# Spreading the sixteen row maxima of an attention step over twelve slots in place of eleven

## The chip, the core and the metric

The kernel runs on one core of a Trainium2 chip. The metric is the device time of one execution in microseconds, lower is better. A core has a matrix engine (TensorE, in the profile PE, its weight loads PEld), a vector engine (VectorE, DVE), an engine for activations (ScalarE, ACT), a general one (GpSimd, POOL) and one that mostly issues DMAs (SyncE, SP). Each has an in-order queue, and they meet through semaphores.

## What is computed

Two attention blocks, one after the other, over x of 16 batches x 512 positions x 512 features, both with float32 inputs. The change lies in the first one, with 16 heads of 32 features:

```python
xn = layer_norm(x, norm_w, norm_b)
q = (xn @ q_w + q_b).reshape(Bx, Tx, H, -1)
k = (xn @ k_w + k_b).reshape(Bx, Tx, H, -1)
att = jnp.einsum('bnhl,bmhl->bnmh', q, k)
att = att + (1.0 - mask) * -1000000.0        # mask over n, the query position
att = jax.nn.softmax(att, axis=2)
v = ((xn @ v_w + v_b) * src_mask[:, :, None]).reshape(Bx, Tx, H, -1)
y = jnp.einsum('bnmh,bmhl->bnhl', att, v).reshape(Bx, Tx, Dx)
```

Behind it come a layer norm of y with a scale and a shift from a condition vector, a silu, an output projection and the residual; the second block is a linear attention.

## The kernel before

Two phases run one behind the other. The first, attention_phase, computes q, k, v, the softmax and its product with v for all 16 batches and writes y to DRAM; the second, projection_phase, does the rest and is not touched.

In the first phase a batch b has four steps g = 0 to 3, each for a group of four heads (HG=4), and a step has 16 slots (SLOTS). The loops over steps are the same on every engine; each engine's queue walks through the same slots and does its own part. A step has these strands:

- **Exponents** (exp_scores, L537): one matmul of 512 columns in a slot, transposed scores, less the row maxima that ride along as two extra rows (the shift rows) of the stacked operand q_stack. ACT exponentiates the bank (L769) into probs. The step's own exponents begin in slot 3 (LAG); slots 0 to 2 finish those of the step before. There are two exp_banks: a matmul waits until ACT has read the one before the last.
- **Maxima for the next step** (max_scores, L522): 16 matmuls, four heads by four tiles of positions. DVE reduces each bank to one column of negmax (maximum, L905). There are two max_banks: matmul m waits for the reduce of m-2. How many fall in which slot is said by maxima(k), the subject of the change: the first of a slot is issued after the exponent matmul, the second after all other work of the slot.
- **The turning of the maxima** (transpose_max, L528): in slot MAX_TURN, after the exponent matmul, PE turns negmax (128x16) into a work bank. It waits for all 16 reduces. DVE splits it in two parts (split_shift, L916 and L918) and SP writes them as the shift rows of the next step (L345), which that step's first exponent waits for in its slot 3.
- **Projections** (project_quarter, L505): q and k for the step after next, a quarter (three matmuls of 512 columns) in each of slots 0 to 3 and 4 to 7. ACT writes the high part of each (L743) and issues two DMAs into the stacks (L750), DVE writes the low part (L891). In the steps g=3 and g=0 two tiles of v as well, one in slots 8, 9, 10 and 10, one (called v') in slots 13, 14, 15 and 15. DVE adds the bias of the first in slot 11, behind the slot's maxima, and of the second at the end of the step (add_value_bias, L900); ACT then multiplies by the mask (L755, the first in slot 12).
- **x of the next batch**, in g=1: DVE normalises it in slots 5 to 8 (L880), PE turns its four tiles in slots 8 to 11 (transpose_x, L512), ACT copies the high part (L737) and DVE takes the low part a slot later (L886).
- **Weighted values** (weigh_values, L548) and **sums** (L560): 16 and 4 short matmuls behind the exponent of slot 9 (two tiles of the step before, and its sums), 16 more behind that of slot 11. The sums use an addition that GpSimd makes (L293).

Projections, turned x and turned maxima take the two work banks in turn, in the order of uses_of. Each use, before its first matmul, waits in take_bank until the use before the last has been read:

```python
if static >= 2:
    pe.wait_ge(work_read, number - 1)
```

In g=0 the order is q, k, v2, m, v3, in g=3 q, k, v0, m, v1, in g=1 q, k, x0 to x3, m, and in g=2 q, k, m (m is the turned maxima). So v3 waits until v2's bias add has read its bank, and in g=1 m waits for the low part of x2.

Of the kernel before, what the change touches and what calls it, by code (L numbers as in the profile page):

```python
# [35 lines left out]
SLOTS = TT * HG  # L36
# [68 lines left out]
def attention_phase(nc, shared, x, mask, mask1, norm_w, norm_b, q_w, q_b, k_w, k_b, v_w, v_b, cond, films, b_vectors,  # L105
# [4 lines left out]
    with ExitStack() as ctx:  # L110
# [126 lines left out]

        QUARTERS = {"q": (0, 1, 2, 3), "k": (4, 5, 6, 7), "v": (8, 9, 10, 10), "v'": (13, 14, 15, 15)}
        X_TURNS = (8, 9, 10, 11)
        MAX_TURN = 12  # L240

        FILM_TURNS = ((4, 6, 8), (6, 8, 12))
        FIRST_V_BIAS = {1: 0, 3: 1, 5: 2, 7: 3}
# [1 line left out]

        def maxima(k):

            return range(min(k * 3 // 2, SLOTS), min((k + 1) * 3 // 2, SLOTS))

        def exp_of(b, g, k):  # L250

# [5 lines left out]
        def use(b, g, what, last=False):  # L257

            n = len(FIRST_USES) + sum(len(uses_of(h, last)) for h in range(g)) + uses_of(g, last).index(what)
            return n, b * USES + n  # L260
# [218 lines left out]
        def _(pe):  # L479
# [35 lines left out]
            def max_scores(b, g, m, first=False):  # L515

                j, nt = m // TT, m % TT
                if m == 0:
                    pe.wait_ge(stack_in[g], DMA * STACK_DMAS * (b + 1))
                if not (first and m < 2):  # L520
                    pe.wait_ge(max_done, SLOTS * step_of(b, g) + m - 1)
                pe.matmul(max_bank[m % 2][:, :], q_stack[0:ROWS_MAX, g, j, nt * P:(nt + 1) * P],  # L522
                          k_stack[0:ROWS_MAX, g, j, :], start=True, stop=True).then_inc(max_full, 1)

            def transpose_max(b, g, number):
                out = take_bank(number)
                pe.wait_ge(max_done, SLOTS * (step_of(b, g) + 1))
                pe.transpose(out[0:SLOTS, 0:P], negmax[:, :], ident[:, :]).then_inc(work_full, 1)  # L528
# [142 lines left out]
            def step(b, g, last=False, first=False):  # L671
# [3 lines left out]
                for k in range(SLOTS):  # L675
# [3 lines left out]
                    if has_next:  # L679
                        for m in maxima(k)[:1]:  # L680
                            max_scores(n_b, n_g, m)
                        if k == MAX_TURN:
                            transpose_max(n_b, n_g, use(b, g, "m", last))
# [31 lines left out]
                    if has_next:  # L715
                        for m in maxima(k)[1:]:
                            max_scores(n_b, n_g, m)
# [145 lines left out]
        def _(dve):  # L863
# [31 lines left out]
            def add_value_bias(b, mt, static, number):  # L895
                dve.wait_ge(work_full, number + 1)
                if not (type(b) is int and b == 0):

                    dve.wait_ge(pv_done, TT * (step_of(b, 0) - 1) + mt + 1)
                dve.tensor_tensor(v_sb[:, mt, :], work_bank[static % 2][:, :], v_bias[:, :], ALU.add  # L900
                                  ).then_inc(work_read, 1)
# [6 lines left out]
            def split_shift(b, g, static, number):  # L908

                s = step_of(b, g)  # L910
                dve.wait_ge(work_full, number + 1)
                if not (type(s) is int and s == 0):

                    p_b, p_g = (b, g - 1) if g else (b - 1, NG - 1)
                    dve.wait_ge(shift_in[p_g], 2 * DMA * (p_b + 1))
                dve.tensor_copy(shift[:, 0, :], work_bank[static % 2][0:SLOTS, 0:P]).then_inc(shift_hi, 1)  # L916
                dve.wait_ge(shift_hi, s + 1)
                dve.tensor_tensor(shift[:, 1, :], work_bank[static % 2][0:SLOTS, 0:P],  # L918
                                  shift[:, 0, :].bitcast(F32), ALU.subtract).then_inc(work_read, 1)
# [105 lines left out]
            def step(b, g, last=False):  # L1025
                has_next = not last or g < NG - 1
                n_b, n_g = (b, g + 1) if g + 1 < NG else (b + 1, 0)
                for k in range(SLOTS):
                    if has_next:
                        for m in maxima(k):  # L1030
                            maximum(n_b, n_g, m)
                    for i, what in enumerate("qk"):
                        if k == QUARTERS[what][-1] + 1 and (not last or g < NG - 2):
                            low_of(what, (g + 2) % NG, use(b, g, what, last)[0], high_count(b, g, i))
                    if g == 1 and not last and 5 <= k < 5 + TT:
                        normalise_x(b + 1, [k - 5])
                    if g == 1 and not last and k - 1 in X_TURNS:
                        tt = X_TURNS.index(k - 1)
                        low_of_x(tt, use(b, 1, f"x{tt}")[0], high_count(b, 1, 2 + tt))
                    if k == 11 and (g == 0 or (g == NG - 1 and not last)):  # L1040
                        mt = 2 if g == 0 else 0
                        add_value_bias(b if g == 0 else b + 1, mt, *use(b, g, f"v{mt}", last))
                    if has_next and k == MAX_TURN:
                        split_shift(n_b, n_g, *use(b, g, "m", last))
                    if g == 0 and not last and k == 13:
                        statistics_of_x(b + 1)
                    if last and g == NG - 2 and k == FILM_TURNS[0][2] + 1:
                        add_film_bias(0, use(b, g, "film0c", last))
                    if last and g == NG - 1:
                        for half in range(2):  # L1050
                            if k == FILM_TURNS[1][half] + 1:
                                copy_film_half(1, half, use(b, g, "film1" + "ab"[half], last))
                        if k == FILM_TURNS[1][2] + 1:
                            add_probs(dve, step_of(b, g), 1)
                            add_film_bias(1, use(b, g, "film1c", last))
                            finish_film()
# [736 lines left out]
def build(nc, i, out):  # L1793

    B = i["x"].shape[0]
    yT_dram = nc.dram_tensor("yT_scratch", (B, D, T), F32, kind="Internal").ap()
    sums_dram = nc.dram_tensor("sums_scratch", (B, NG * HG, T), F32, kind="Internal").ap()
    mb0_dram = nc.dram_tensor("mask_bias0_scratch", (B, 2, T), F32, kind="Internal").ap()
    mb1_dram = nc.dram_tensor("mask_bias1_scratch", (B, T), F32, kind="Internal").ap()
    mask1 = i["mask_BxSx1_fk1"].rearrange("b t o -> b (t o)")  # L1800
    films = [tuple(i[layer + n] for n in names) for layer, names in
             (("L0_cond_", ("emb_w", "emb_b", "sb_norm_w", "sb_norm_b")), ("L1_cond_", ("W_emb", "b_emb", "ln2_w", "ln2_b")))]
    b_vectors = films[0][1:] + films[1][1:] + (i["L1_cond_ln_w"], i["L1_cond_ln_b"], i["L1_cond_bk"])
    with ExitStack() as ctx:
        shared = Shared(nc, ctx, B)
        attention_phase(nc, shared, i["x"], i["mask_BxS_ff1"], mask1, i["L0_cond_norm_w"], i["L0_cond_norm_b"],
                        i["L0_cond_q_w"], i["L0_cond_q_b"], i["L0_cond_k_w"], i["L0_cond_k_b"], i["L0_cond_v_w"],
                        i["L0_cond_v_b"], i["cond_2048"], [film[0] for film in films], b_vectors,
                        yT_dram, sums_dram, mb0_dram, mb1_dram)
        projection_phase(nc, shared, i["x"], i["L0_cond_out_w"], i["L0_cond_out_b"], i["L1_cond_Wq"], i["L1_cond_bq"],  # L1810
                         i["L1_cond_Wk"], i["L1_cond_Wv"], i["L1_cond_bv"], i["L1_cond_W_out"], i["L1_cond_b_out"],
                         yT_dram, sums_dram, mb1_dram, out)
# [17 lines left out]
```

## Time and profile before

| what | value |
|---|---|
| time, median of 3 runs | 2792.67 us (2791.71 to 2795.97) |
| profiled execution, its own time | 2797.07 us |
| its span | 2795.2 us |
| PE busy | 2672.4 us, 96% |
| DVE busy | 1827.3 us, 65% |
| POOL busy | 1352.2 us, 48% |
| ACT busy | 1223.7 us, 44% |
| mean granted clock of PE | 0.982 |

The profile is of one execution. Busy time counts overlapping stretches of an engine once; matmuls are pipelined, so the start times of two neighbours say more of their cost than their durations (0.40 us each where they start 0.23 us apart). The first phase ends at about 1541 us of the span.

### The profile page before, as it was taken

What the parts mean: (1) busy time and instruction counts of PE and PEld (TensorE: products, weight loads), DVE (VectorE), ACT (ScalarE), POOL (GpSimd) and SP (SyncE); (2) the same over time, 40 slices, a digit from 0 to 9 for tenths busy, and PEclk for the clock granted to TensorE, in tenths of its full rate; (3) what the DMA queues carried; (4) which work ended last, traced back from release to release, by engine and by line L of the source; (5) the groups of instructions that cost most, each with busy time, mean ns of one, the idle gap of its engine ahead of it and who ended that gap; (6) DMA issues with size and microseconds to landing.
All of it is one profiled execution on the core that took longest, in us unless ns stands there. A gap on an engine that the chain in (4) does not pass through costs nothing. (4 is left out here: it accounts for less than half of the span.)

```text
span 2795.2 us, 43889 instructions
## 1 busy us (share of the span) xinstructions
PE 2672.4 (96%) x13890; PEld 1947.1 (70%) x13890; DVE 1827.3 (65%) x3272; ACT 1223.7 (44%) x2039; POOL 1352.2 (48%) x604
## 2 busy tenths in 40 slices
PE   7999999999999999999998699999999999999997
PEld 4666556665666666666663488888888888888886
DVE  6766666666665666666653666666677776776674
ACT  3555555555555555555554323333333333333332
POOL 1656566656666665666564234433333333343432
PEclk9999999999999999999998699999999999999998
DMA  6656665666566656666564411111111111111100
GB/s 138 100 79 99 99 99 78 99 99 99 78 98 98 97 80 96 96 95 95 81 99 137 145 35 50 49 49 49 49 49 47 48 45 37 43 45 49 34 30 31
DMA packets 114915, 211.44 MB, mean 76 GB/s; under 512 B 12408, under 2 KB 14508, under 8 KB 114876
## 3 DMA queue, kind: packets, MB, share of 16 engines
q1 hardware_dynamic: 78012, 143.81, 22.3%
q10 hardware_dynamic: 36864, 67.13, 18.2%
q8 instruction: 22, 0.36, 0.1%
q14 instruction: 17, 0.14, 0.0%
HBM read 74.87 MB, written 34.18 MB: 39 GB/s over the span
## 5 line engine op out<-in xcount | busy, mean ns | idle before, releaser
L905 DVE TENSOR_REDUCE negmax<-max_bank 128x1 f32<-128x512 f32 x1024 | 682.1, 687 | 330.2 <-PE max_bank L522 328.7
L769 ACT ACTIVATE probs<-exp_bank 128x512 f32<-128x512 f32 x1024 | 586.8, 596 | 538.0 <-PE exp_bank L537 484.6
L293 POOL TENSOR_TENSOR probs_sum<-probs_sum,probs 128x2048 f32<-128x2048 f32 x126 | 581.0, 4611 | 73.6 <-ACT probs L769 69.5
L293 POOL TENSOR_TENSOR probs_sum<-probs 128x2048 f32<-128x2048 f32 x63 | 288.4, 4577 | 541.1 <-ACT probs L769 541.1
L537 PE MATMUL exp_bank<-q_stack,k_stack 100*128 100x512 f32 x1024 | 432.5, 432 | 24.5 <-ACT probs L769 21.8
L522 PE MATMUL max_bank<-k_stack,q_stack 98*128 98x512 f32 x1024 | 421.4, 416 | 21.6 <-DVE negmax L905 12.6
L537 PEld LDWEIGHTS exp_bank<-q_stack,k_stack 100*128 100x128 f32 x1024 | 193.5, 189 | 171.2 <-ACT probs L769 85.3
L522 PEld LDWEIGHTS max_bank<-k_stack,q_stack 98*128 98x128 f32 x1024 | 192.7, 190 | 139.2 <-issue 59.3
L1528 POOL TENSOR_TENSOR sT_lo<-silu,sT_hi 128x512 fp32r<-128x512 f32 x128 | 173.0, 1372 | 175.2 <-DVE sT_hi L1643 175.2
L548 PE MATMUL y_bank<-probs,v_sb 128*32 128x512 f32 x2048 | 248.0, 602 | 0.0
L1309 PE MATMUL b_work<-ident,area 128*128 128x128 f32 x1536 | 193.0, 281 | 25.1 <-DMA b_sums<-sums_scratch 13.3
L1283 PE MATMUL b_work<-b_wout_hi,sT_hi 128*128 128x512 f32 x512 | 201.8, 394 | 9.5 <-issue 5.0
L1309 PEld LDWEIGHTS b_work<-ident,area 128*128 128x128 f32 x1536 | 176.1, 145 | 39.4 <-DMA b_sums<-sums_scratch 14.3
L1283 PE MATMUL b_work<-b_wout_lo,sT_hi 128*128 128x512 f32 x512 | 201.1, 393 | 0.0
L1283 PE MATMUL b_work<-b_wout_hi,sT_lo 128*128 128x512 f32 x512 | 201.1, 393 | 0.0
L1523 POOL TENSOR_TENSOR rstd_y<-var_eps_y,b_minus_half 128x4 f32<-128x4 f32 x32 | 32.8, 1024 | 334.1 <-DVE var_eps_y L1607 334.1
L1643 DVE CAST sT_hi<-silu 128x512 fp32r<-128x512 f32 x128 | 102.1, 818 | 104.0 <-ACT silu L1468 104.0
L1507 ACT ACTIVATE area<-area 128x512 f32<-128x512 f32 x64 | 40.4, 632 | 274.6 <-POOL area L1573 274.6
L1468 ACT ACTIVATE silu<-b_work,film_b,film_a 128x512 f32<-128x512 f32 x128 | 93.2, 777 | 128.7 <-PE b_work L1309 101.2
L1543 POOL TENSOR_TENSOR result<-area,row_out 128x512 f32<-128x512 f32 x64 | 82.8, 1304 | 125.9 <-DMA out_x<-result 125.9
L548 PEld LDWEIGHTS y_bank<-probs,v_sb 128*32 128x32 f32 x2048 | 53.6, 109 | 120.0 <-issue 112.7
L1494 ACT ACTIVATE area<-area,kmax 128x512 f32<-128x512 f32 x64 | 46.0, 720 | 196.8 <-DVE kmax L1669 196.6
(194 smaller groups left out, 5290.1 us busy)
## 6 DMA issues: line engine op xcount, KB each, us to landing
q_stack<-q_stage ACTq DMA_DIRECT2D x128, 256.0 KB
k_stack<-k_stage ACTq DMA_DIRECT2D x128, 256.0 KB
x_sb<-in_x SPq DMA_DIRECT2D x16, 1024.0 KB, 5.6
q_stack<-q_stage SPq DMA_DIRECT2D x64, 256.0 KB
k_stack<-k_stage SPq DMA_DIRECT2D x64, 256.0 KB
yT_scratch<-y_stage SPq DMA_DIRECT2D x64, 256.0 KB
area<-yT_scratch SPq DMA_DIRECT2D x16, 1024.0 KB, 5.2
area<-in_x SPq DMA_DIRECT2D x64, 256.0 KB, 2.8
```

The lines of the kernel that those rows point to most:

```text
L293: eng.tensor_tensor(probs_sum[:, :, :], so_far, probs[:, mt, :, :], ALU.add).then_inc(probs_added, 1)
L522: pe.matmul(max_bank[m % 2][:, :], q_stack[0:ROWS_MAX, g, j, nt * P:(nt + 1) * P], k_stack[0:ROWS_MAX, g, j, :], start=True, stop=True).th ...
L537: pe.matmul(exp_bank[k % 2][:, :], k_stack[0:ROWS_EXP, g, j, mt * P:(mt + 1) * P], q_stack[0:ROWS_EXP, g, j, :], start=True, stop=True).th ...
L548: last = pe.matmul(y_bank[DH0 * j:DH0 * (j + 1), :], v_sb[:, mt, P * j + DH0 * g:P * j + DH0 * (g + 1)], probs[:, mt, j, :], start=(mt == ...
L769: act.activation(probs[:, mt, j, :], exp_bank[k % 2][:, :], ACT.Exp).then_inc(exp_done, 1)
L905: dve.tensor_reduce(negmax[:, m:m + 1], max_bank[m % 2][:, :], AXX, ALU.max, negate=True).then_inc(max_done, 1)
L1283: last = pe.matmul(out, lhs(a, kt), rhs(c, kt), start=(kt == 0 and a + c == 0), stop=(kt == KT - 1 and a == 1))
L1309: last = pe.transpose(out[:, i * P:(i + 1) * P], src(i), ident[:, :])
L1468: act.activation(silu[:, kt % SILUS, :], bank(u), ACT.Silu, scale=film_columns(film_a[film], kt, row), bias=film_columns(film_b[film], kt, ...
L1528: pool.tensor_tensor(sT_lo[:, kt, :], silu[:, kt % SILUS, :], sT_hi[:, kt, :].bitcast(F32), ALU.subtract).then_inc(sT_lo_done, 1)
L1543: pool.tensor_tensor(result[:, tt, :], x_sb[:, tt, :], rows["out1"][:, :], ALU.add).then_inc(result_biased, 1)
L1643: dve.tensor_copy(sT_hi[:, kt, :], silu[:, kt % SILUS, :]).then_inc(sT_hi_done, 1)
```

## The change

Two lines of attention_phase. maxima(k) gave slots 0 to 10 the counts 1,2,1,2,1,2,1,2,1,2,1; it gives slots 0 to 11 the counts 1,1,2,1,1,2,1,1,2,1,1,2. The maxima are turned in slot 13 in place of 12. Both PE and DVE take their order from these lines.

```diff
-        MAX_TURN = 12
+        MAX_TURN = 13
...
         def maxima(k):
 
-            return range(min(k * 3 // 2, SLOTS), min((k + 1) * 3 // 2, SLOTS))
+            return range(min(k * 4 // 3, SLOTS), min((k + 1) * 4 // 3, SLOTS))
```

## Rows read from the trace of the kernel before

**Rows 1.** The page: PE's busy time, and the granted clock by slice.

```profile
PE 2672.4 (96%) x13890; PEld 1947.1 (70%) x13890; DVE 1827.3 (65%) x3272; ACT 1223.7 (44%) x2039; POOL 1352.2 (48%) x604
...
PEclk9999999999999999999998699999999999999998
```

**Rows 2.** Windows of steps g=0 to 3: busy us of each engine, clock, DMA share.

```profile
520.36:544.33 23.97, 23.97 (x123) 15.96 (x122) 16.36 (x31) 12.71 (x22) 13.84 (x4) 1.00 0.56 79
544.33:567.79 23.46, 21.57 (x115) 12.97 (x113) 17.80 (x31) 13.09 (x24) 13.81 (x5) 1.00 0.56 79
567.79:588.05 20.26, 19.43 (x97) 11.42 (x97) 12.44 (x20) 11.05 (x19) 13.70 (x3) 1.00 0.64 85
588.05:612.02 23.97, 23.96 (x121) 16.04 (x122) 13.15 (x21) 12.27 (x21) 14.88 (x5) 1.00 0.69 129
```

**Rows 3.** Timeline of PE in step g=0: start us, us, engine, line, operation.

```profile
520.36 0.40 PE L537 MATMUL exp_bank<-q_stack,k_stack 100*128 100x512 f32 x1
...
525.03 0.39 PE L505 MATMUL work_bank<-xT_hi,wq_lo 128*128 128x512 f32 x1
...
528.15 0.49 PE L537 MATMUL exp_bank<-q_stack,k_stack 100*128 100x512 f32 x1
...
540.31 0.50 PE L537 MATMUL exp_bank<-q_stack,k_stack 100*128 100x512 f32 x1
540.65 0.27 PE L528 MATMUL work_bank<-ident,negmax 128*16 128x128 f32 x1
...
540.99 0.40 PE L505 MATMUL work_bank<-wv_hi,xT_hi 128*128 128x512 f32 x1
...
544.33 0.40 PE L537 MATMUL exp_bank<-q_stack,k_stack 100*128 100x512 f32 x1
```

**Rows 4.** Timeline of DVE in the same step: last reduces, bias add.

```profile
536.50 1.29 DVE L905 TENSOR_REDUCE negmax<-max_bank 128x1 f32<-128x512 f32 x2 [0.24 <-PE max_bank L522]
538.45 0.69 DVE L900 TENSOR_TENSOR v_sb<-work_bank,v_bias 128x512 f32<-128x512 f32 x1 [0.67 <-PE work_bank L505]
```

**Rows 5.** Timeline of ACT in the same step, slots 4 to 6.

```profile
527.50 1.78 ACT L769 ACTIVATE probs<-exp_bank 128x512 f32<-128x512 f32 x3 [1.35 <-PE exp_bank L537]
```

**Rows 6.** Timeline of PE in steps g=1 and g=2.

```profile
555.71 0.50 PE L522 MATMUL max_bank<-k_stack,q_stack 98*128 98x512 f32 x1 [0.31 <-DVE negmax L905]
...
559.53 0.50 PE L522 MATMUL max_bank<-k_stack,q_stack 98*128 98x512 f32 x1
...
562.09 0.66 PE L512 MATMUL work_bank<-ident,x_sb 128*128 128x128 f32 x4 [0.78 <-DVE xT_lo L886]
...
564.76 0.66 PE L512 MATMUL work_bank<-ident,x_sb 128*128 128x128 f32 x4
...
567.79 0.50 PE L537 MATMUL exp_bank<-q_stack,k_stack 100*128 100x512 f32 x1 [0.20 <-ACT probs L769]
...
581.87 0.74 PE L522 MATMUL max_bank<-k_stack,q_stack 98*128 98x512 f32 x2
...
583.15 0.50 PE L522 MATMUL max_bank<-k_stack,q_stack 98*128 98x512 f32 x1 [0.31 <-DVE negmax L905]
...
585.68 0.50 PE L537 MATMUL exp_bank<-q_stack,k_stack 100*128 100x512 f32 x1
...
588.05 0.50 PE L537 MATMUL exp_bank<-q_stack,k_stack 100*128 100x512 f32 x1 [0.19 <-ACT probs L769]
```

**Rows 7.** Timeline of DVE in steps g=1 and g=2.

```profile
561.35 0.68 DVE L886 TENSOR_TENSOR xT_lo<-work_bank,xT_hi 128x512 fp32r<-128x512 f32 x1
...
582.41 1.98 DVE L905 TENSOR_REDUCE negmax<-max_bank 128x1 f32<-128x512 f32 x3 [1.91 <-PE max_bank L522]
```

**Rows 8.** The shift rows' DMAs (L345), all 128: issue to landing.

```profile
DMA to landing us min/median/max: 1.8/1.9/9.1
```

**Rows 9.** Windows over one PV product each, at the two granted clocks.

```profile
1537.00:1540.40 3.40, 3.40 (x17) 0.74 (x20) 2.47 (x2) 0.73 (x2) 0.00 (x0) 0.50 0.00 0
538.40:540.30 1.90, 1.90 (x17) 0.42 (x16) 0.69 (x1) 1.08 (x2) 1.90 (x1) 1.00 0.49 79
```

## Prediction

> **What bounds the kernel now.** I read the page's busy shares first, then its 40 slices. TensorE (PE) is busy for 96% of the span and holds nine tenths or more in nearly every slice at the full granted clock [rows 1]. So a microsecond counts only if it adds work to PE's queue or holds that queue up. The windows of the four group steps of one middle batch come next [rows 2]: 23.97 us (g=0), 23.46 (g=1), 20.26 (g=2) and 23.97 (g=3), with PE busy all through the first and the last, and idle 1.89 and 0.83 us in the others. The two long steps carry the V tiles (I call them V steps), g=1 the turning of x, g=2 neither. The change touches these steps alone, some 62 of them. The second phase, after about 1550 us, is untouched.
>
> Then the order of time on PE within a V step [rows 3]. Streaming matmuls start 0.2335 us apart: 20 of them lie between 520.36 and 525.03. I call this a unit. Slots 12 to 15 run from 540.31 to 544.33: the exponent matmul of slot 12 is at 540.31, the turning of the maxima at +0.34 with no idle time shown before it, the first V' matmul at +0.68, and the next step's first matmul at +4.02. The turning waits for nothing because its last maximum was computed in slot 10, and slot 11's PV product (16 short matmuls, from 538.4 to 540.3 in the second of [rows 9]) gave VectorE (DVE) 1.9 us to reduce it. DVE had finished its reduces by 537.79 and the V bias add by 539.14 [rows 4], before the turning.
>
> **What the change does to the order.** Before, slots 0 to 10 compute 1,2,1,2,1,2,1,2,1,2,1 maxima. After, slots 0 to 11 compute 1,1,2,1,1,2,1,1,2,1,1,2. Nothing is added or removed: 16 max matmuls, 16 reduces, one turning, the split and two shift rows remain. What moves: slots 0 to 7 hold 10 maxima in place of 12; slots 8 to 10 hold four both times; slot 11 now holds maxima 14 and 15, and they are issued behind its PV product. Slot 12 has a single exponent matmul, and the turning stands behind slot 13's. The cover of the PV product is gone. On DVE, whose queue is in order, the reduces of 14 and 15 now stand ahead of slot 11's V bias add (V steps) and of the low part of x2 (g=1).
>
> **The tail of a V step.** Let P be the time at which PE is through slot 11's PV product, 540.31 in rows 3. Max 14 starts at P and max 15 a wait-free 0.33 later. The same pair behind a long product is seen in g=2 (x2 in one row): first matmul at 581.87 [rows 6], first reduce at 582.41 [rows 7], 0.54 later. Two back-to-back reduces take 1.29 [rows 4], so the second ends at P+1.83. A waiting PE goes on 0.06 after DVE ends: the low part ends at 562.03 [rows 7] and the matmul behind it starts at 562.09 [rows 6]. The turning therefore starts at P+1.89, not P+0.34. PE has only the two max and two exponent matmuls to do before (to about P+1.1).
>
> Worse stands behind it. V' goes into the work bank that the earlier V tile used, which is free only when the bias add has read it. That add now starts one pitch after the second reduce. Of two reduces in 1.29 with 0.69 each the second starts 0.60 after the first, so the add starts at P+0.54+1.20 = P+1.74 and takes 0.69 (the add in rows 4): it ends at P+2.43, and V' starts at P+2.49. From V' to the next step PE took 544.33-540.99 = 3.34 [rows 3]. The next step starts at P+5.83 where it was P+4.02: **+1.81**, the two moved matmuls (0.47 of work) included. ScalarE (ACT) has the mask multiply of slot 12 behind the same add, to about P+3.2, then exponent 13 to P+3.7. PE wants that bank in slot 15, at P+4.15, so this second wait stays covered.
>
> **What slots 0 to 7 give back.** Two matmuls fewer are 0.47. But PE's exponent of slot 6 already waits for ACT: the last q matmul is at 525.03, the q high part and its DMA issues hold ACT, slot 4's exponential starts at 527.50 [rows 5] and ends near 528.09, and PE goes on at 528.15 [rows 3], 3.12 us after 525.03 where 13 units are 3.04. One of the two maxima leaves exactly that stretch: 12 units are 2.80 and the exponent still can't start before 3.12. It only makes the wait longer. The other leaves slots 6 and 7, where nothing waits. So 0.24 comes back. **V step: 1.81-0.24 = +1.57.** The 16 steps g=0 and 15 of g=3 have V: 31 x 1.57 = **+48.7 us**.
>
> **g=2.** Slots 0 to 7: -0.24. Slot 8 gets a second max, +0.23. Behind the sums PE did max 13, max 14, exponent 10, max 15 and exponent 11 in slots 9 and 10. Max 15 came at 583.15 [rows 6], behind a wait for the reduce of max 13. Now these are max 12, exponent 10, max 13 and exponent 11, with no pair and no wait: 0.33 and two units, 0.80 from the first to exponent 11. Before it was 583.15+0.34-581.87 = 1.62. That is -0.82. P itself is thus earlier by 0.83. In the tail the turning starts at P+1.89 again and slot 14's exponent behind it at P+1.93. Its ACT pass starts 0.54 later, takes 0.60, and the next step's first exponent, which wants the same bank, starts at P+3.1; before, 588.05-585.68 = 2.37. That is +0.73. **-0.10 each, 15 times: -1.5 us**.
>
> **g=1.** Slots 0 to 7: -0.24, and some 0.16 less of short waits for DVE. Slot 8 loses a wait for DVE of 0.31 (555.71 [rows 6], some 0.37 with what a stop costs beside it) and gains one matmul behind a turning (0.30). Behind the sums (Q = 559.53) the turning of x2 waited for DVE until Q+2.56, because reduces 13 and 14 stood ahead of x0's low part. Now one reduce does: it ends at Q+1.2, the low part at Q+1.83, x2 starts at Q+1.89: -0.67. In the tail the turning needs the bank that x2's low part frees, now behind both reduces. With x3 between them, max 15 is at P+0.73, its reduce ends at P+1.89, the low part at P+2.5, the turning starts at P+2.56, and the next step at P+3.8 by the same chain as in g=2; before, 567.79-564.76 = 3.03. That is +0.77. **-0.37 each, 15 times: -5.6 us**. The last batch's g=1 and g=2 I take as zero.
>
> **Where the shift rows go.** Their two DMAs follow the split on SP's queue, with nothing between, and land in 1.9 us [rows 8]. They are wanted in slot 3. In g=2 I estimate the turning at P+1.89, the split and the two issues 1.8 us more, the landing near P+5.6; slot 3's exponent comes 16 units after the step's first, at P+6.8. In the V steps it comes at P+9.6, with over 3 us to spare. So they cost nothing. GpSimd (POOL) adds the exponentials somewhat later, but PE wants these sums only behind slot 9 of the next step.
>
> **Sum.** 48.7-1.5-5.6 = +41.6 us. The profiled execution took 2797.07 us (span 2795.2), 4.4 above the median of 2792.67; from it 2838.7, and from the median **2834.3 us**, 1.5% slower. About 0.2% is what a measurement can tell here.
>
> **Bounds.** A V step: +1.2 if slots 0 to 7 give back the full 0.47 and slot 15's small wait goes too; +1.9 if nothing comes back. g=1: -0.8 to 0. g=2: -0.4 to +0.3. Low: 31x1.2-15x1.2 = +19; high: 31x1.9+15x0.3 = +63.
>
> **Rivals.** (a) *The late reduce is covered and the smoother order wins.* If the turning and V' found DVE ready, the tails would cost only the moved matmuls (0.47 each), and per batch the rest gives 0.24+0.24+1.24+0.83 = 2.55 against 4x0.47 = 1.88: -0.67, times 15.5 is -10 us, 2782. It decides if DVE's second reduce and the add end before about P+1.1. Rows 6 and 7 speak against it: 0.54 and 1.29 can't fit. 4%. (b) *The V bank is not what V' waits for*, and the turning alone costs: V' then comes 0.34 behind it, at P+2.23, the V step is +1.31, and the sum 31x1.31-7 = +34, 2826. It decides if the bias add is through by P+2.2. In rows 4 add and reduces are far apart, so no row shows their pitch; 12%. *An exact cancel* has half of (a)'s gap closed, 3%. (c) *The shift rows come late* in g=1 and g=2, where cover is 0.9 to 1.2 us. Landing took up to 9.1 us at worst [rows 8]. One us over the cover in both is 30 us more, 2864. The rows' DMAs meet little traffic at the step's end, hence 4%. (d) *The clock falls.* At the lower granted level 17 matmuls of PV take 3.40 us, at full 1.90 [rows 9]. If the 14 matmuls behind the wait ran so in each V step: 31x3.3 = 102 us more, 2937. Against it: g=1 idles 1.89 us at 1.00 [rows 2], and the longest new gap is about 1. 2%. The Trainium skill's page "TensorE: Matmul & The Clock Gate", section "HAM oscillation — how this bites in real kernels", warns that waits between bursts of matmuls can throttle the clock again and again; the trace of this stage doesn't show that, and the sum above leaves it out. The forecast has 75%.
>
> **Range.** 2814 to 2852 leaves out (a), the cancel, (c) and (d), and holds (b). Faster 0.04, same 0.03, slower 0.93.
>
> **What would show it.** Windows of the four steps near 25.5, 23.1, 20.2 and 25.5 us. L528 no longer free of idle time but released by the DVE reduce L905 (g=0,2,3) or the low part L886 (g=1); V' matmuls (L505) released by DVE L900; the DVE wait at max 15 and most of the x2 wait gone; the exponent of slot 6 waiting some 0.3 us for ACT; the split L916 some 1.5 us or more after exponent 13. It would be wrong if V steps stay under 24.5, or if PE waits for the shift DMA in every batch.

## The result

The changed kernel takes 2852.97 us (median of 4 runs, 2850.51 to 2855.16) against 2792.19 us for the kernel before: ratio 1.0215, 95% interval 1.0197 to 1.0232, 60.8 us slower. I had forecast 2834.3 us with a range up to 2852.0. The direction was right, the size 18.7 us short, and the time lies just outside the range. Each time here and below is the median of a kernel's undisturbed runs; two of the twelve of experiment 9, at 3785 and 5289 us, are left out.

### The profile page after: what moved, and what is told of

It is laid out like the page before. It is cut to its first block and busy times, and to the rows that moved or that the text cites. A ratio compares the mean times of both kernels' runs of the same rounds, so it can differ in the third digit from the quotient of the medians.

```text
span 2852.8 us, 43889 instructions
## 1 busy us (share of the span) xinstructions
PE 2684.6 (94%) x13890; PEld 1953.7 (68%) x13890; DVE 1824.6 (64%) x3272; ACT 1225.1 (43%) x2039; POOL 1351.4 (47%) x604
## 5 line engine op out<-in xcount | busy, mean ns | idle before, releaser
L905 DVE TENSOR_REDUCE negmax<-max_bank 128x1 f32<-128x512 f32 x1024 | 690.3, 688 | 524.1 <-PE max_bank L522 523.4
L537 PE MATMUL exp_bank<-q_stack,k_stack 100*128 100x512 f32 x1024 | 413.9, 420 | 28.6 <-ACT probs L769 25.5
L1309 PEld LDWEIGHTS b_work<-ident,area 128*128 128x128 f32 x1536 | 176.1, 145 | 39.2 <-DMA b_sums<-sums_scratch 14.3
```

The source lines that it names most:

```text
L537: pe.matmul(exp_bank[k % 2][:, :], k_stack[0:ROWS_EXP, g, j, mt * P:(mt + 1) * P], q_stack[0:ROWS_EXP, g, j, :], start=True, stop=True).th ...
L905: dve.tensor_reduce(negmax[:, m:m + 1], max_bank[m % 2][:, :], AXX, ALU.max, negate=True).then_inc(max_done, 1)
L1309: last = pe.transpose(out[:, i * P:(i + 1) * P], src(i), ident[:, :])
```

## The profile after

The page's busy shares and slices, as in [rows 1]:

```profile
PE 2684.6 (94%) x13890; PEld 1953.7 (68%) x13890; DVE 1824.6 (64%) x3272; ACT 1225.1 (43%) x2039; POOL 1351.4 (47%) x604
...
PEclk9999999999999999999999699999999999999998
```

The work is the same to the instruction, the span 57.6 us longer (2852.8), so the difference is waiting or clock. The slices of the clock look as before; at 70 us each they hide what follows. Windows of the steps g=0 to g=3 of one batch, with a second g=2 at the end (span us, then busy us of each engine with counts, granted clock, DMA share, GB/s), as in [rows 2]:

```profile
538.82:564.52 25.70, 24.55 (x122) 15.91 (x121) 16.50 (x31) 12.87 (x22) 13.79 (x4) 1.00 0.52 74
564.52:587.44 22.92, 20.84 (x114) 12.74 (x113) 17.47 (x29) 13.02 (x24) 13.58 (x5) 1.00 0.58 80
587.44:609.12 21.68, 20.41 (x97) 12.51 (x97) 12.47 (x20) 10.99 (x20) 13.75 (x3) 0.92 0.60 79
609.12:634.90 25.78, 24.61 (x122) 16.14 (x123) 13.16 (x21) 12.34 (x21) 15.18 (x4) 1.00 0.67 120
...
492.79:513.00 20.21, 18.93 (x97) 11.38 (x97) 12.46 (x20) 11.01 (x20) 13.77 (x3) 1.00 0.64 84
```

The two V steps are 1.7 to 1.8 us longer than in [rows 2], g=1 is 0.5 us shorter, an undisturbed g=2 nearly as long as before (20.21 against 20.26 us). But one g=2 took 21.68 us, at a mean granted clock of 0.92. That wasn't in my sum.

The tail of a V step on PE (start us, us, engine, line), to hold against [rows 3]:

```profile
556.83 1.92 PE L548 MATMUL y_bank<-probs,v_sb 128*32 128x512 f32 x16
558.68 0.73 PE L522 MATMUL max_bank<-k_stack,q_stack 98*128 98x512 f32 x2
559.26 0.63 PE L537 MATMUL exp_bank<-q_stack,k_stack 100*128 100x512 f32 x2
560.57 0.28 PE L528 MATMUL work_bank<-ident,negmax 128*16 128x128 f32 x1 [0.68 <-DVE negmax L905]
561.16 0.50 PE L505 MATMUL work_bank<-wv_hi,xT_hi 128*128 128x512 f32 x1 [0.32 <-DVE v_sb L900]
...
564.52 0.40 PE L537 MATMUL exp_bank<-q_stack,k_stack 100*128 100x512 f32 x1
```

and on DVE in the same stretch, to hold against [rows 4]:

```profile
559.22 1.29 DVE L905 TENSOR_REDUCE negmax<-max_bank 128x1 f32<-128x512 f32 x2 [3.21 <-PE max_bank L522]
560.43 0.68 DVE L900 TENSOR_TENSOR v_sb<-work_bank,v_bias 128x512 f32<-128x512 f32 x1
```

P is 558.68. The first reduce starts at P+0.54, the turning at P+1.89, V' at P+2.48, the next step at P+5.84. The forecast had 0.54, 1.89, 2.49 and 5.83. The two brackets are the two stops of the forecast. DVE, which had been done before P, now has three operations in a row there, and PE waits for the second and the third.

Where the forecast was off in a V step lies ahead of P. The exponents of slots 2 and 6 on PE, to hold against [rows 3]:

```profile
540.92 0.40 PE L505 MATMUL work_bank<-xT_hi,wq_lo 128*128 128x512 f32 x1
541.20 0.50 PE L537 MATMUL exp_bank<-q_stack,k_stack 100*128 100x512 f32 x1
541.53 0.39 PE L522 MATMUL max_bank<-k_stack,q_stack 98*128 98x512 f32 x1
...
543.63 0.39 PE L505 MATMUL work_bank<-xT_hi,wq_lo 128*128 128x512 f32 x1
...
546.20 0.39 PE L522 MATMUL max_bank<-k_stack,q_stack 98*128 98x512 f32 x1
546.74 0.50 PE L537 MATMUL exp_bank<-q_stack,k_stack 100*128 100x512 f32 x1 [0.16 <-ACT probs L769]
```

and on ACT:

```profile
544.77 1.21 ACTq L750 DMA_DIRECT2D q_stack<-q_stage  x2
546.09 1.79 ACT L769 ACTIVATE probs<-exp_bank 128x512 f32<-128x512 f32 x3 [1.35 <-PE exp_bank L537]
```

The maximum and the exponent of slot 6 start 0.54 us apart where streaming takes 0.23: PE waits for the exponential that stands behind the two DMA issues. From the step's first matmul to P it was 540.31-520.36 = 19.95 before [rows 3] and is 558.68-538.82 = 19.86: the two missing maxima give back 0.09, not 0.24. Slot 6 isn't the reason: its exponent starts 3.11 us behind the last q matmul (546.74-543.63), where the forecast had 3.12. The missing 0.15 lies in slot 2. Its exponent starts 0.28 behind the matmul ahead of it, and the next one 0.33 behind it, where streaming takes 0.23 each. In the kernel before one maximum more stood ahead of it, and it streamed:

```profile
522.93 0.40 PE L537 MATMUL exp_bank<-q_stack,k_stack 100*128 100x512 f32 x1
523.17 0.39 PE L522 MATMUL max_bank<-k_stack,q_stack 98*128 98x512 f32 x1
```

The stop in g=1, and what came behind it:

```profile
583.62 0.50 PE L522 MATMUL max_bank<-k_stack,q_stack 98*128 98x512 f32 x1
583.95 0.60 PE L512 MATMUL work_bank<-ident,x_sb 128*128 128x128 f32 x4
584.31 0.48 PE L522 MATMUL max_bank<-k_stack,q_stack 98*128 98x512 f32 x1
584.63 0.63 PE L537 MATMUL exp_bank<-q_stack,k_stack 100*128 100x512 f32 x2
586.25 0.27 PE L528 MATMUL work_bank<-ident,negmax 128*16 128x128 f32 x1 [0.99 <-DVE xT_lo L886]
586.28 0.71 PE L537 MATMUL exp_bank<-q_stack,k_stack 100*128 100x512 f32 x2
587.44 0.50 PE L537 MATMUL exp_bank<-q_stack,k_stack 100*128 100x512 f32 x1 [0.45 <-ACT probs L769]
...
588.84 0.63 PE L505 MATMUL work_bank<-xT_hi,wq_lo 128*128 128x512 f32 x1
589.26 0.63 PE L537 MATMUL exp_bank<-q_stack,k_stack 100*128 100x512 f32 x1
...
591.39 0.42 PE L537 MATMUL exp_bank<-q_stack,k_stack 100*128 100x512 f32 x1
```

P is 583.62 here. The turning starts at P+2.63 (forecast 2.56), the next step at P+3.82 (3.8). From about 588.0 the matmuls start 0.42 to 0.43 us apart until 591.39. A window over that stretch:

```profile
588.00:591.40 3.40, 3.40 (x10) 2.62 (x9) 1.39 (x2) 1.17 (x2) 3.40 (x1) 0.51 0.04 10
```

The granted clock is at its lower level, 1.2 GHz. PE had stopped twice just before, for 0.99 and 0.45 us. In the stretch from 100 us to 1480 us the changed kernel shows ten such falls of 3.4 us, the kernel before none. (In the last batch, which has less work, both kernels show one of 10.2 us. In the kernel before it begins at 1486.2 us, behind a wait of 2.86 us for a stack.) Seven of the ten lie behind the tail of g=1, three behind that of g=2, none behind a V step, and a step that has one is 1.5 us longer (g=2 21.71 against 20.18). The tail of a g=2 has two stops as well, the first of them shorter:

```profile
607.92 0.28 PE L528 MATMUL work_bank<-ident,negmax 128*16 128x128 f32 x1 [0.67 <-DVE negmax L905]
...
609.12 0.50 PE L537 MATMUL exp_bank<-q_stack,k_stack 100*128 100x512 f32 x1 [0.43 <-ACT probs L769]
```

The count is of the one execution that was profiled. The mean granted clock of the changed kernel's four runs is 0.977 to 0.979, that of experiment 7, which has no such fall, 0.983 to 0.985. From this I estimate some 8 to 12 falls in each run.

The balance, from the lengths of all steps in the trace (here and in the experiments from the first maximum of a step to that of the next, which differs from the windows by up to 0.1 us): V steps 31 x 1.71 = 53.0; g=1 15 x -0.52 = -7.8; g=2 15 x -0.09 = -1.4; ten falls x 1.5 = 15.0. That is 58.8 of a difference of 57.6 us; the small rest is at the start and end of the phase.

## The experiments

The theory: a V step pays for the last two reduces and the bias add once PV no longer covers them, and the stops of g=1 and g=2 let the clock fall. The rivals: the turning's place costs by itself; the spread costs by itself; the falls have another reason.

**1. The turning in slot 13 alone**, on the kernel before.

```diff
-        MAX_TURN = 12
+        MAX_TURN = 13
```

> Kernel before, with the turning moved to slot 13 alone; the maxima stay in eleven slots. Theory (the order of the last two maxima and the PV product is what costs): reduce 15 is through long before slot 13, so no wait, V steps stay at 23.97 us, the time at 2792 us within 5, and the granted clock does not fall in the middle of the first phase. Rival (a turning one slot later costs by itself, through the bank or the shift rows): 10 us or more slower.

Measured: 2793.59 us, ratio 1.0001 (0.9990 to 1.0011). V steps 23.97 and 23.99 us, no fall of the clock between 100 and 1480 us. The second line of the change costs nothing.

**2. The spread alone**, the turning left in slot 12.

```diff
         def maxima(k):
-            return range(min(k * 3 // 2, SLOTS), min((k + 1) * 3 // 2, SLOTS))
+            return range(min(k * 4 // 3, SLOTS), min((k + 1) * 4 // 3, SLOTS))
```

> The new spread with the turning left in slot 12. Theory: the turning waits until the same moment (1.9 us behind the PV product) but exponent 13 now stands behind it; V steps stay at 25.7 us (V' waits for its bank anyway), g=1 and g=2 are 0.6 us longer each, some 18 us over the changed kernel, 2871 us, and the granted clock falls at least as often. Rival (the wait is the turning's place, not the maxima's): faster than the changed kernel.

Measured: 2853.37 us, ratio 1.0213 (1.0196 to 1.0231), as slow as the whole change. The steps are as expected, V steps 25.6 to 25.7, g=1 23.55 and g=2 20.7, which is 0.5 us more each. But the clock fell twice, not ten times, which gives back nearly all of that; here the expectation missed. So the slot of the turning decides nothing about the V steps: both stops come from where the last two maxima stand. And a longer stop doesn't bring more falls: the turning of g=1 waits 1.22 us here, that of g=2 0.91, and the stop behind each is 0.45 and 0.46 as before.

**3. PV behind slot 11's maxima.** The new spread and slot 13 stay; PE issues the product last in its slot.

```diff
@@ exp_slot
-                if e == 8:
-                    weigh_values(b, g, 0)
-                    weigh_values(b, g, 1)
@@ step, behind the second maximum of the slot
+                    if k == LAG + 8:
+                        weigh_values(b, g, 0)
+                        weigh_values(b, g, 1)
```

> The new spread and slot 13, but on PE slot 11's PV product is issued behind that slot's maxima instead of ahead of them. Theory: the product covers the reduces of 14 and 15 again, no wait before the turning or V', V steps 23.9 us, g=1 23.1, g=2 20.5 (max 15 now waits for reduce 13), no fall of the clock in the phase: 2787 us. Rival (the spread itself costs, whatever stands behind it): near the changed kernel, 2840 or more.

Measured: 2802.05 us, ratio 1.0032 (1.0021 to 1.0042). 51 of the 61 us are gone with one moved product. The turning waits no more, and the clock doesn't fall before the last batch. The line of the turning:

```profile
L528 PE MATMUL work_bank<-ident,negmax x64: 269/273/273, 63.8 to 1517.7; 128*16 128x128 f32 x64
its engine sat idle before it (us, times) until:
  issue: 0.6, 1
  DVE negmax L905: 0.2, 1
```

In the changed kernel the same row says 99.7 us of idle time in 105 intervals (weight load and matmul counted apart) until DVE's reduces and 16.1 until the low part. Still it is 8 us slower than the kernel before, measured beside it (2793.94), and 15 us slower than I expected. The V steps are 24.42 and 24.26 us, not 23.9; g=1 is 22.99 and g=2 20.65 us. A part of that is my slip: I counted what slots 0 to 7 give back and not the 0.47 us that the same two matmuls take in slot 11. The window of one:

```profile
522.58:547.00 24.42, 24.26 (x123) 15.84 (x122) 16.26 (x28) 12.70 (x22) 13.82 (x4) 1.00 0.55 78
```

Slots 0 to 7 take 10.40 us with 42 matmuls here (522.58 to 532.98) and took 10.46 with 44 before. The smoother order gives almost nothing back in a V step even where its tail is covered. So rival (a) doesn't come true here; experiment 8 shows what it takes.

**4. The bias add ahead of the reduces** on DVE in slot 11; all else as changed.

```diff
                 for k in range(SLOTS):
+                    if k == 11 and (g == 0 or (g == NG - 1 and not last)):
+                        mt = 2 if g == 0 else 0
+                        add_value_bias(b if g == 0 else b + 1, mt, *use(b, g, f"v{mt}", last))
                     if has_next:
                         for m in maxima(k):
                             maximum(n_b, n_g, m)
...
-                    if k == 11 and (g == 0 or (g == NG - 1 and not last)):
-                        mt = 2 if g == 0 else 0
-                        add_value_bias(b if g == 0 else b + 1, mt, *use(b, g, f"v{mt}", last))
```

> The changed kernel with DVE's slot 11 bias add ahead of the slot's reduces. Theory: V' no longer waits for its bank but follows the turning at P+2.23 in place of P+2.48, V steps 25.45 us, 8 us less in all, 2845 us. If the bank wait were the larger part of a V step's loss: 30 us less.

Measured: 2838.68 us, ratio 1.0162 (1.0145 to 1.0180), 14.3 us less than the changed kernel. V steps are 25.16 to 25.23 us, 0.5 shorter and not 0.25. The falls of the clock are ten, as in the changed kernel. PE in the tail:

```profile
554.12 0.28 PE L528 MATMUL work_bank<-ident,negmax 128*16 128x128 f32 x1 [0.67 <-DVE negmax L905]
554.21 0.49 PE L505 MATMUL work_bank<-wv_hi,xT_hi 128*128 128x512 f32 x1
```

V' starts 0.09 behind the turning, not 0.34. The bank wait is real and its own; I had under-priced it, because the 0.34 from the turning to V' in [rows 3] had an exponent matmul in it as well.

**5. x2's low part ahead of the reduces** on DVE in g=1.

```diff
                 for k in range(SLOTS):
+                    if g == 1 and not last and k == 11:
+                        low_of_x(2, use(b, 1, "x2")[0], high_count(b, 1, 4))
                     if has_next:
                         for m in maxima(k):
                             maximum(n_b, n_g, m)
...
-                    if g == 1 and not last and k - 1 in X_TURNS:
+                    if g == 1 and not last and k - 1 in X_TURNS and k != 11:
```

> The changed kernel with x2's low part ahead of slot 11's reduces on DVE, in g=1. Theory: the turning in g=1 then waits for the reduces alone, P+1.95 in place of P+2.63, and the step is 0.4 us shorter, 6 us in all. If the long stop in g=1 is what lets the clock fall, the ten falls in the middle of the phase go too: 15 us more, 2832 us. Rival (the falls come from the stops as a whole): falls stay near ten, 2847 us.

Measured: 2837.29 us, ratio 1.0164 (1.0146 to 1.0183). g=1 is 22.52 us, 0.5 shorter. The whole is 15.7 us below the changed kernel. Of the falls four are left, all behind g=2 and none behind g=1. So the shorter stop in g=1 ends the falls there, but not those behind g=2: between the theory and the rival. The four runs lie 11 us apart, and the slowest (2845.13 us) has a lower mean clock (0.978) than the profiled one (0.981), so it most likely has more falls.

**6. Unused matmuls in g=1's stop.** They need no bank that is in use and take no wait away.

```diff
+                        if k == MAX_TURN and g == 1 and not last:
+                            pe.wait_ge(max_done, SLOTS * step_of(n_b, n_g) + SLOTS - 1)
+                            for _ in range(4):
+                                pe.matmul(max_bank[0][:, :], q_stack[0:ROWS_MAX, n_g, 0, 0:P],
+                                          k_stack[0:ROWS_MAX, n_g, 0, :], start=True, stop=True)
                         if k == MAX_TURN:
                             transpose_max(n_b, n_g, use(b, g, "m", last))
```

> The changed kernel with four unused matmuls (scores into max bank 0, which the next step overwrites) ahead of the turning in g=1, after the reduce of maximum 14; they fit into the stop and take no wait away. Clock theory: TensorE is busier there, no falls to the lower clock in the middle of the phase, g=1 stays at 23.06 us, 15 us less, 2838 us. Rival (the falls have another reason, or cost nothing): 2853 us or slightly more.

The stop filled, from PE's timeline (the four are L685):

```profile
581.34 0.64 PE L537 MATMUL exp_bank<-q_stack,k_stack 100*128 100x512 f32 x2
581.82 1.09 PE L685 MATMUL max_bank<-k_stack,q_stack 98*128 98x512 f32 x4
582.97 0.27 PE L528 MATMUL work_bank<-ident,negmax 128*16 128x128 f32 x1
```

Measured: 2841.77 us, ratio 1.0167 (1.0151 to 1.0183). The turning is still at P+2.63 and g=1 at 23.05 us. No fall is left behind g=1, but six are there behind g=2, where there had been three. Adding work took 11 us away. The profiled run is the slowest of the four (2844.42 us).

**7. The same in g=1 and g=2** (four and two matmuls):

```diff
-                        if k == MAX_TURN and g == 1 and not last:
+                        if k == MAX_TURN and g in (1, 2) and not last:
...
-                            for _ in range(4):
+                            for _ in range(4 if g == 1 else 2):
```

> The changed kernel with four unused matmuls in the stop before the turning of g=1 and two in that of g=2. With fillers in g=1 alone the falls behind g=1 were gone and six came behind g=2. Clock theory: none is left in the middle of the phase, every step takes its undisturbed length (25.7, 23.05, 20.18, 25.7 us), 2838 us. Rival (the falls only move to another place, the V steps): six or more stay, 2842 us or slower.

Measured: 2838.29 us, ratio 1.0168 (1.0151 to 1.0185). There is no fall between 100 and 1500 us; the steps are 25.7, 23.06, 20.17 and 25.67 us in every batch. With every wait in place the falls alone were worth 2852.97-2838.29 = 14.7 us. What is left is 4 us from my forecast.

**8. ACT's stack DMAs one exponential later**, with PV behind the maxima as in experiment 3.

```diff
                             high_of(what, (g + 2) % NG, number, static)
+                        if k == QUARTERS[what][-1] + 1 and (not last or g < NG - 2):
                             stack_high(what, (g + 2) % NG, high_count(b, g, "qk".index(what)))
```

> The new spread with the PV product behind slot 11's maxima, and in addition ACT issues the two stack DMAs of q and k one exponential later. Theory: in slots 0 to 7 PE waits in slot 6 for the exponential that stands behind ACT's DMA issues, and this wait eats what two fewer maxima give back (slots 0 to 7 took 10.40 us with 42 matmuls, 10.46 with 44). Without it each step is 0.3 us shorter, 19 us in all: 2783 us. Rival (something else holds slots 0 to 7): no change from 2802.

Measured: **2780.60 us, ratio 0.9952 (0.9940 to 0.9964)**, faster than both kernels, and 21.5 us less than experiment 3. V steps 23.93 and 23.85 us, g=1 23.0, g=2 20.2. The exponent of slot 6 had been held by the exponential that stands behind two DMA issues on ACT (1.21 us), and this wait had eaten the gain: slots 0 to 7 of a step g=0 now take 9.95 us, not 10.41. g=1 gains nothing by the move. It was already nearly 0.6 us shorter than in the kernel before in experiment 3, and at 15 steps this is some 8 of the 12 us that the new order is now ahead.

**9. The same on the kernel before.**

> The kernel before with ACT's two stack DMA issues one exponential later. Theory: its wait in slot 6 is only 0.09 us and a dearer start behind it, so 5 us less, 2788 us. Rival (the later stacks are then waited for by the next step): slower.

Measured: 2790.45 us, ratio 0.9993 (0.9984 to 1.0002): no difference that can be measured. Steps are shorter by 0.03 to 0.09 us. The move is worth something only where the spread has made the wait large.

**10. The same on the changed kernel.**

> The changed kernel with ACT's stack DMA issues one exponential later, PV product where the change leaves it. Theory: slots 0 to 7 give back what the two missing maxima are worth, each of the steps is 0.4 us shorter, some 25 us in all, V steps 25.25 us: 2828 us, with the stops of the tail and about as many falls of the clock unchanged. Rival (the gain was special to the kernel without stops in the tail): 2850 us.

Measured: 2851.23 us, ratio 1.0210 (1.0193 to 1.0227), 1.7 us less and not 25. V steps did fall, to 25.26 us, 0.43 x 31 = 13 us. g=1 and g=2 kept their length. Behind g=2 the next step's first maximum now waits for the stack that is loaded later:

```profile
608.38 0.49 PE L522 MATMUL max_bank<-k_stack,q_stack 98*128 98x512 f32 x1 [0.24 <-DMA k_stack<-k_stage]
```

In g=1 slots 0 to 7 do take 0.4 us less, but in slot 8 PE then waits for a reduce: the second maximum starts 0.71 us behind the turning of x ahead of it, where it had been 0.35. And the clock fell in fifteen places, three of them (all behind g=2) for twice as long, where it had been ten. That took back nearly all of what the V steps gave. A gain ahead of a stop can be lost in it.

## Why the prediction was right and wrong

*The tail of a V step* was right to 0.02 us at each of its four points. Its source in the order, the last two maxima behind PV, is shown by experiments 1 to 3. *The split of that loss* between turning and bank was off: the bank add is worth 0.5 us a step (experiment 4), so rival (b)'s price was wrong too, though the sum of both was right.

*"So 0.24 comes back"* failed in size. The wait for ACT in slot 6 came as foreseen (3.11 against 3.12 us), and experiments 3 and 8 show that moving the DMA issues removes it. But in the V step shown 0.09 came back. With one maximum less ahead of it, the exponent of slot 2 in g=0 meets ACT, which is still at the exponentials behind the mask multiply of g=3's second V tile; this costs 0.15 us, which I had not counted. In g=3 the last q matmul comes 0.09 late, nearly all of it in slot 0. At +1.71 against +1.57, 31 steps make 4.3 us.

*g=2* was right (-0.09 against -0.10). *g=1* was -0.52 against -0.37, 2 us in all: slots 0 to 7 gave back 0.29 and not 0.40, but the waits in slot 8 and ahead of x2 shrank by 0.3 more than I had put.

*The shift rows* hid as forecast: two exponents in the whole run waited for them, 2.9 us together (one before, 2.3 us).

*The clock* is the step that failed: the sum had nothing for it. Rival (d) got 2% with the reason "g=1 idles 1.89 us at 1.00 [rows 2], and the longest new gap is about 1". The stop did come out at 0.99 us. The reason was wrong: g=1 idles 2.08 us now (22.92-20.84), hardly more than before. The sum over a step says nothing of it. Before, the x2 stop of 0.78 us [rows 6] stood ahead of a PV product; now the stops stand close together at the end of the step, and the clock falls right behind. That this place makes the difference is my reading; no run tests it by itself. I also looked for the fall in V steps, where V' work follows and it never came. Its real form is ten falls that cost 1.5 us each, 15 us of the 19 that were missing. Experiments 6 and 7, which add work in the stops and take less time, show that filling the idle time there ends the falls. The Trainium skill, page "TensorE: Matmul & The Clock Gate", section "HAM oscillation — how this bites in real kernels", tells of a clock that is throttled anew in every round of a loop, behind waits for DMA. The loss here is of that kind, but the waits are for other engines and last at most 1 us, shorter than those that the section describes, and the clock falls in some rounds only; what was measured here decides. The prediction says that the trace of this stage doesn't show such a thing; it did show one fall, in the last batch.

*The range* was narrower than its own bounds. They add up to +63 us, which is 2855.8, but the range ended at 2852 without a reason. The wider one would have held the result by luck, for none of its terms was the clock. In rival (a) the 1.24 us of g=1 should be 1.14 by the terms given, 1.6 us in all.

Open: why only some batches show a fall, and why experiment 2, with longer stops, has two where the changed kernel has ten and experiment 10 fifteen. The runs don't tell.

## What to carry to other kernels

Work that another engine must finish before the next step should be issued ahead of the long product, not behind it: the same matmuls in the same slot cost 51 us less when they stand in front of PV. Where two engines run in lock step, evening out one engine's load gives nothing if its next wait grows by the same amount, so look for the wait first (here the one behind two DMA issues in ACT's queue). When a change opens stops of under a microsecond, look at the granted clock stretch by stretch after it, not at the mean or at 40 slices.

## What I had not expected of the hardware

TensorE fell from 2.4 to 1.2 GHz for 3.4 us behind pairs of stops of 0.99 and 0.45 us, and three times behind 0.67 and 0.43 us, while it was 94% busy over the phase (1221.8 of 1300 us). Four unused matmuls in the longer stop (1.09 us of work that ends before the wait does) keep the clock up there, and six in a batch make the whole 14.7 us faster than leaving the engine idle.
